# Full attention in a four-stage transformer kernel: rows of tiles taken from last to first, sums of masked values made beforehand, and masks and normalisation moved to GpSimd

## The reference

```python
def _scaled_dot_product_attention(q, k, v):
    scores = jnp.einsum('bqd,bkd->bqk', q, k) / jnp.sqrt(jnp.float32(d_k))
    scores = jnp.triu(scores, k=0)
    scores = jnp.where(scores == 0, MASK_NEG, scores)      # -9e15
    attn = jax.nn.softmax(scores, axis=-1)
    return jnp.einsum('bqk,bkd->bqd', attn, v)
x = x + _L0_attn_b_ref(_layernorm(x, axis=-1), L0_attn_b_W)      # one head of 128
# _L0_ffn_ref, routing part
probs = jax.nn.softmax(xf @ w_router, axis=-1)
topk_w, topk_idx = jax.lax.top_k(probs, TOP_K)
```

## Time and profile before

| what | us |
|---|---|
| median of three runs | 1597.03 |
| profiled execution | 1602.1 |
| its span, first to last instruction | 1600.3 |
| TensorE busy, 9684 matmuls | 1295.0 (81%) |
| VectorE busy | 1071.1 (67%) |
| ScalarE busy | 909.5 (57%) |
| GpSimd busy | 789.2 (49%) |
| norm 2: first transfer to the first projection of the attention | 1055.14 to 1097.13 |
| full attention, first projection to first load of the experts | 1097.13 to 1396.68 |

### The profile page before, as it was taken

One profiled execution on the slowest core, in us unless ns is written; L12 is line 12 of the kernel. 1 busy time (PEld: TensorE's weight loads), 2 busy tenths in 40 slices (PEclk: granted clock), 3 DMA queues, 4 the chain that ended last, 5 costly groups with the idle time before them and its releaser, 6 DMA issues. The chain is left out here.

```text
span 1600.3 us, 34684 instructions
## 1 busy us (share of the span) xinstructions
PE 1295.0 (81%) x9684; PEld 1015.8 (63%) x9684; DVE 1071.1 (67%) x3751; ACT 909.5 (57%) x2312; POOL 789.2 (49%) x814
## 2 busy tenths in 40 slices
PE   0699999999999999999982888916977886188891
PEld 0467666766766776676661888903765666188890
DVE  5666776877877788776864455556886878445563
ACT  1277777768777686767752544513764666044450
POOL 4357667676676857757672354510022223434451
PEclk9899999999999999999995989957999899598996
DMA  5699995000000000000004112130000000121215
GB/s 191 117 206 198 204 203 107 1 7 7 4 11 0 15 1 7 8 2 13 1 14 135 56 57 59 55 105 0 1 14 14 14 18 25 35 65 52 62 55 158
DMA packets 129390, 91.84 MB, mean 57 GB/s; under 512 B 9115, under 2 KB 122030, under 8 KB 128992
## 3 DMA queue, kind: packets, MB, share of 16 engines
q1 hardware_dynamic: 118848, 71.32, 20.3%
q0 software_dynamic: 9248, 16.94, 3.2%
q10 hardware_dynamic: 1152, 2.13, 0.4%
HBM read 30.86 MB, written 61.64 MB: 58 GB/s over the span
## 5 line engine op out<-in xcount | busy, mean ns | idle before, releaser
L812 DVE CUSTOM_DVE_ANT_0 sc<-ps,mask 128x256 f32<-128x256 f32 x518 | 198.6, 420 | 161.4 <-PE ps L627 137.8
L734 ACT ACTIVATE sc<-sc,mx 128x256 f32<-128x256 f32 x516 | 256.9, 501 | 40.0 <-DVE mx L812 39.4
L962 POOL TENSOR_TENSOR rot<-rot,sin 128x512 f32<-128x512 f32 x132 | 183.6, 1391 | 191.0 <-DVE rot L821 191.0
L1109 POOL DMA_INDIRECT yt<-yo,xt x160 | 160.3, 1002 | 197.5 <-DVE yo L1209 167.4
L441 POOL DMA_INDIRECT xg<-r_xw,r_slot x128 | 127.2, 994 | 170.7 <-DVE r_slot L418 136.1
L742 ACT COPY pT<-pt 128x512 f32<-128x512 f32 x257 | 150.1, 584 | 103.2 <-PE pt L637 95.2
L627 PE MATMUL ps<-K,Q 64*128 64x256 f32 x1036 | 193.1, 435 | 15.2 <-DVE mx L812 15.2
L1169 ACT ACTIVATE hT<-ph,b 128x256 f32<-128x256 f32 x320 | 125.4, 475 | 86.5 <-PE ph L1132 86.5
L637 PE MATMUL pt<-ident,sc 128*128 128x128 f32 x1028 | 171.3, 290 | 1.5 <-ACT sc L734 1.3
L650 PE MATMUL po<-pT,V 128*64 128x128 f32 x2048 | 171.5, 289 | 0.0
L637 PEld LDWEIGHTS pt<-ident,sc 128*128 128x128 f32 x1028 | 109.7, 142 | 86.2 <-issue 57.6
(11 more groups left out here) (236 smaller groups left out, 2767.9 us busy)
## 6 DMA issues: line engine op xcount, KB each, us to landing
xg<-zeros SPq DMA_DIRECT2D x76, 520.0 KB, 10.8
xt<-xg SPq DMA_DIRECT2D x80, 130.0 KB, 2.1
got<-yt SPq DMA_DIRECT2D x32, 256.0 KB, 4.5
yt<-yo,xt POOLq DMA_INDIRECT x160, 2.3
x<-in_hidden SPq DMA_DIRECT2D x8, 256.0 KB, 8.1
xg<-r_xw,r_slot POOLq DMA_INDIRECT x128, 2.3
w<-in_w SPq DMA_DIRECT2D x1, 2048.0 KB, 8.7
out_x<-x SPq DMA_DIRECT2D x8, 256.0 KB, 4.0
```

The costliest lines, as they stand in the source:

```text
L734: nc.scalar.activation(sc[:, b, h, :], sc[:, b, h, :], ACT.Exp, scale=-1.0, bias=mx[:, b, h:h + 1], accum_out=ls[:, c % 2, b, h:h + 1]).th ...
L812: nc.vector.tensor_tensor_reduce(sc[:, b, h, :], ps[:, h, 0:2 * P], (mask0 if b == 0 else mask)[:, :], -float(HD) ** -0.5, 3e38, ALU.add, ...
L962: nc.gpsimd.tensor_tensor(rot[:, which, :], rot[:, which, :], s.sin[:, pos(sb)], ALU.mult).then_inc(S["pool"], 1)
L1109: nc.gpsimd.indirect_dma_start(out=s.yt, out_offset=bass.IndirectOffsetOnAxis(ap=xt[:, k, r, HID:HID + 1].bitcast(U32), axis=0), in_=yo[:, ...
```

## The change

Five things change, nearly all in the full attention.

- Rows run from the last to the first: r = 0 is row i = 15, with one tile. The groups of 512 tokens are finished and routed from the last to the first of each sequence (`where`). ROUTE_AT is set anew.
- The sums of masked values are made once per batch, before the rows. TensorE makes four products of ones with all the values (projections 12 to 15), VectorE adds them up to the sums `pre` of all 16 rows (`sums`). TensorE adds a row's part to `bpo` by one product of `diag`, the identity times the weights `w0`, with `pre`. VectorE's `finish` is a reciprocal and an update straight from PSUM.
- GpSimd masks the first tile of a row (`mask`) and makes `diag` (`weigh`), with waits on ScalarE's copy and weights; VectorE's take then waits for the mask. With one chunk in a row the second reduction is left out.
- GpSimd normalises a group for the routing (`normalise_on_pool`); VectorE only sends the reciprocal (`invert`). Its scatters are spread over four chunks, two at a time.
- Two groups share a semaphore for fetched outputs, so `combine` waits for the transfers of both.

```diff
-            sp.dma_start(got[:, k, r, :], parts[k][:, r, :]).then_inc(s.fetched[i], 16)
+            sp.dma_start(got[:, k, r, :], parts[k][:, r, :]).then_inc(s.fetched[i // 2], 16)
...
-    ch.eng.wait_ge(s.fetched[i], 16 * TOPK * nth)
+    ch.eng.wait_ge(s.fetched[i // 2], 32 * TOPK * nth)
...
-        return self.s.x[:, bass.ds(g * SB_TILES + t, 1), :].rearrange("p o d -> p (o d)")
+        return self.s.x[:, bass.ds(self.where(g) * SB_TILES + t, 1), :].rearrange("p o d -> p (o d)")
...
+    def invert(self, dve, g):
+        self.hold(dve, self.S["std"], START + g + 1)
+        self.nc.vector.reciprocal(self.rstd[:, :], self.tmp[:, 0, :]).then_inc(self.S["rs"], 1)
+
+    def normalise_on_pool(self, pool, g):
+
+        pool.wait_ge(self.S["rs"], START + g + 1)
+        if g >= self.bufs:
+            pool.wait_ge(self.put[self.buf(g)], 16 * TOPK * SB_TILES * (g // self.bufs))
+        for t in range(SB_TILES):
+            ins = self.nc.gpsimd.tensor_scalar(self.xw[:, self.buf(g), 0, t, 0:HID], self.tile(g, t),
+                                               self.mean[:, t:t + 1], self.rstd[:, t:t + 1], ALU.subtract, ALU.mult)
+        ins.then_inc(self.S["xn"], 1)
...
-        rt = Router(nc, m, s, 3, 2, 0)
+        rt = Router(nc, m, s, 3, 2, 0, lambda j: BTILES // SB_TILES * (j // 4) + 3 - j % 4)
...
-        pre = m.sb("pre", [P, HID + 1])
-        oo = m.sb("oo", [P, HID + 1])
+        pre = m.sb("pre", [P, BTILES, HID + 1])
+        diag = m.sb("diag", [P, DBUF, P])
...
-        chunks = [[(k, min(4, BTILES - k)) for k in range(i, BTILES, 4)] for i in range(BTILES)]
-        first = [sum(len(c) for c in chunks[:i]) for i in range(BTILES + 1)]
+        rows = [(BTILES - 1 - r, [(k, min(4, BTILES - k)) for k in range(BTILES - 1 - r, BTILES, 4)])
+                for r in range(BTILES)]
+        first = [sum(len(chunks) for _, chunks in rows[:r]) for r in range(BTILES + 1)]
         NCH = first[-1]
...
         ROUTE_AT = [first[4 * j % BTILES + 4] + 1 + NCH * (j // 4) for j in range(NSB)]
-        ROUTE_AT[3], ROUTE_AT[7] = NCH + 5, 2 * NCH + 2
-        END, MORE = 2 * NCH, 9
-        STATS, ROOT, NORMALISE, TURN, LOGITS, EXPS, CHOOSE, SUM, COUNT, SLOTS = 0, 0, 1, 2, 3, 3, 4, 5, 6, 6
+        ROUTE_AT[3], ROUTE_AT[4], ROUTE_AT[5], ROUTE_AT[7] = NCH + 3, NCH + 10, NCH + 17, 2 * NCH + 1
+        END, MORE = 2 * NCH, 12
...
+                for a in range(16):
                     if a >= 2:
-                        k = min(a - 1, 8)
-                        pe.wait_ge(S["qk"], START + 8 * b + k)
-                        if a - 1 > 8:
-                            pe.wait_ge(S["v"], START + 4 * b + a - 9)
+                        pe.wait_ge(S["qk"], START + 8 * b + min(a - 1, 8))
+                    if 10 <= a < 14:
+                        pe.wait_ge(S["v"], START + 4 * b + a - 9)
+                    if a >= 14:
+                        pe.wait_ge(S["pre"], START + 4 * b + a - 13)
                     if a < 2:
-                        pe.wait_ge(S["pre_sb"], START + (BTILES - 1) * b)
+                        pe.wait_ge(S["pre"], START + 4 * b)
+                    if a == 12:
+                        pe.wait_ge(S["v"], START + 4 * (b + 1))
+                        for g in range(AHEAD):
+                            scores(g)
                     sl = slice(a % 4 * SB, (a % 4 + 1) * SB)
                     if a < 8:
...
+                    elif a >= 12:
+                        g = a % 4 * SB_TILES
+                        ins = nc.tensor.matmul(pp[:, a % 2, :], s.ones[:, :], V[:, g:g + SB_TILES, 0:HID],
+                                               start=True, stop=True)
...
+                        ins = nc.tensor.matmul(po[:, r % 2, 0:HID + 1], pT[:, g % 2, t, :], V[:, k0 + t, :],
+                                               start=(c == 0 and t == 0), stop=False)
+                    if c == len(rows[r][1]) - 1:
+                        pe.wait_ge(S["pre"], START + 4 * (b + 1))
+                        pe.wait_ge(S["diag"], START + BTILES * b + r + 1)
+                        ins = nc.tensor.matmul(po[:, r % 2, 0:HID + 1], diag[:, r % DBUF, :], pre[:, i, :],
+                                               start=False, stop=True)
                     ins.then_inc(S["pv"], 1)
 
...
-                    i, c, _, _ = chunk[g]
-                    if c == 0 and i > 0:
-
-                        pe.wait_ge(S["pre_sb"], START + (BTILES - 1) * b + max(i - 2, 0))
-                        nc.tensor.matmul(pp[:, i % 2, 0:HID + 1], s.ones[:, :], V[:, i - 1, :], start=True,
-                                         stop=True).then_inc(S["pre"], 1)
...
-                    ch.wait()
+                    dve.wait_ge(S["o"], START + 4 * (j + 1))
...
-                    rt.normalise(dve, j)
+                    rt.invert(dve, j)
...
+                def sums(a):
+
+                    dve.wait_ge(S["proj"], START + 16 * b + a + 1)
+                    for t in range(SB_TILES):
+                        i = a % 4 * SB_TILES + t
+                        if i < BTILES - 1:
+                            ins = nc.vector.tensor_tensor(pre[:, i + 1, 0:HID], pre[:, i, 0:HID],
+                                                          pp[:, a % 2, t * P:(t + 1) * P], ALU.add)
+                            ch.link(ins)
+                    dve.sem_inc(S["pre"], 1)
...
+                    if c == 0:
+                        dve.wait_ge(S["tri"], START + 2 + BTILES * b + r + 1)
                     to = U[:, g % UBUF, 0:n * P]
-                    if c == 0:
-
-                        ch.link(nc.vector.tensor_tensor(to[:, 0:P], to[:, 0:P], tri[:, :], ALU.mult))
...
+                    last = c == len(rows[r][1]) - 1
+                    least = mn[:, r % UBUF, c:c + 1]
+                    ins = nc.vector.tensor_reduce(least, to, AX_X, ALU.min)
...
+                def finish(r):
+
+                    i = rows[r][0]
+                    dve.wait_ge(S["pv"], START + NCH * b + first[r + 1])
+                    ch.link(nc.vector.reciprocal(st[:, r % UBUF, 3:4], po[:, r % 2, HID:HID + 1]))
                     own = s.x[:, b * BTILES + i, :]
-                    ch.mark(nc.vector.scalar_tensor_tensor(own, oo[:, 0:HID], st[:, i % UBUF, 3:4], own,
-                                                           ALU.mult, ALU.add))
+                    nc.vector.scalar_tensor_tensor(own, po[:, r % 2, 0:HID], st[:, r % UBUF, 3:4], own,
+                                                   ALU.mult, ALU.add).then_inc(S["o"], 1)
...
                     take(g)
+                for a in range(12, 16):
+                    sums(a)
...
+                    rt.normalise_on_pool(pool, j)
+                    rt.second(pool, j)
+                for t in range(SB_TILES):
+                    for j in at(b, g, SCATTER + t):
+                        rt.scatter(pool, j, (t,))
+
+            for b in range(BATCH):
+                def mask(g):
+
+                    r, i, c, k0, n = chunk[g]
+                    if c == 0:
+                        pool.wait_ge(S["copy"], START + NCH * b + g + 1)
+                        of = U[:, g % UBUF, 0:P]
+                        nc.gpsimd.tensor_tensor(of, of, tri[:, :], ALU.mult).then_inc(S["tri"], 1)
+
+                def weigh(g):
+
+                    r, i, c, k0, n = chunk[g]
+                    if c == 0:
+                        pool.wait_ge(S["w0"], START + BTILES * b + r + 1)
+                        if BTILES * b + r >= DBUF:
+                            pool.wait_ge(S["o"], START + BTILES * b + r - DBUF + 1)
+                        nc.gpsimd.tensor_scalar(diag[:, r % DBUF, :], s.ident[:, :], st[:, r % UBUF, 2:3], None,
+                                                ALU.mult).then_inc(S["diag"], 1)
+
+                for g in range(AHEAD - 1):
+                    mask(g)
+                weigh(0)
+                for g in range(NCH):
+                    if g + AHEAD - 1 < NCH:
+                        mask(g + AHEAD - 1)
+                    if g + 1 < NCH:
+                        weigh(g + 1)
+                    route(b, g)
+            for g in range(NCH, NCH + MORE):
+                route(1, g)
             rt.scattered(pool)
 
```

115 lines of the change are left out of this document (48 added, 67 removed).

## The result

The changed kernel takes 1644.9 us by the median of four runs, against 1598.6 us before in the same session: a ratio of 1.0292, 95% interval 1.0257 to 1.0327. (One of the four was a disturbed run of 4155.4 us; the other three are 1638.2 to 1645.7, and the ratio rests on these.) The direction was forecast, +46 us instead of +16 was not, and 1645 lies outside the range that ended at 1629.

What follows compares the result with a forecast made beforehand. In full attention TensorE was taken to set the pace in undisturbed rows, time coming only from batch starts, routing stops and tail. Terms 10.8 + 4.3 + 3.6 - 0.9 - 6.0 + 4.2 = +16.0 on 1597.0 gave 1613 us, range 1588 to 1629.

Steps and rivals of the forecast that it cites:

- (a): Start of a batch: TensorE's first transpose comes 5.4 us later in each of two batches, +10.8 us.
- (c): Stops at routing: shorter root, count and slot stops against GpSimd's normalisation and new places of routings, +3.6 us in sum.
- (b): Work inside the loops: nine more tiles of scores in each loop, diagonal products replacing ones products, +4.3 us.
- The price of a routing in long rows: Full attention: root stop 3.53 us, half clock 1.6, count wait 2.1, slots about 0.8; called about 8.4 us.
- (e): Between batches: the projections no longer wait for the running sum, -0.9 us.
- (d): Masks and weights on GpSimd: masks taken at 0.5 us, weights 0.3, with slack to spare, so 0 us.
- (f): Tail behind the last value product: less row work ahead of the last group's statistics, -6.0 us.
- (g): One semaphore for two groups of fetched results: later adds in the norm stage and at the end, +4.2 us.
- The second, GpSimd as the bound: Rival: GpSimd ends each routing late, eight routings cost 2 us each, +16, 1629 us; chance 0.12.
- the two signs that I named against myself: Prediction wrong if loops take less than 101 and 109 us, or if VectorE's takes wait for masks.
- The first, VectorE as what TensorE waits for: Rival: count and slot stops go, roots shrink, less half clock, start with +2.5; 1587 us; chance 0.22.
- The third: Rival: shorter routing stops keep the clock, 1.6 us go in each of seven routings, -11, 1602 us; chance 0.18.

Runs made afterwards that it cites:

- e6: Against e3, the 15 sums of a batch's start moved between VectorE's first takes, two ones products ahead of TensorE's first scores: 1613.5 us.
- e11: e3 plus sums moved as in e6, later routing steps, and separate signals for the first and last fetched groups: 1604.6 us.
- e1: The changed kernel with the four normalisation passes of a group back on VectorE: 1623.9 us.
- e3: The changed kernel with both masks and normalisation back on VectorE; GpSimd keeps weights, second copy and spread scatters: 1614.8 us.
- e2: The changed kernel with the 32 masks back on VectorE, normalisation and weights staying on GpSimd: 1640.2 us.
- e10: e3 with rows from first to last and routings where the kernel before the change has them: 1609.6 us.
- e9: The changed kernel with routing steps further apart: root one chunk later, turning two chunks behind normalisation, count and slots three later: 1620.1 us.

## Why the prediction was wrong, step by step

**(a) start, +10.8: right** (+12.0). The first transposes came 28.7 and 25.5 us after the first projections, 27.5 and 25 forecast, behind two ones products that waited 3.7 us for VectorE at the most. Its condition also showed: the second of them runs at the lower clock (1.19 and 1.06 us for its two halves, 0.59 undisturbed), in the second batch both. What the step lacked is that in reversed rows this time is not for sale; e6 and e11 moved it into the loops.

**(c), the term "GpSimd normalises, +0.5 at each turning, +3.5": this is the step that failed.** Measured: the waits for the turning go from 2.9 to 23.9 us in the loops, and giving the normalisation back takes 16.8 us out of the loops and 2.2 out of the tail (e1). Two things were mis-sized. The pass costs 0.84 us (0.78 with nothing beside it), not 0.29 to 0.5: I took a copy and a share of a two-input product for an operation that the trace of before did not have on GpSimd, a product with two operands per partition, and called them bounds. By the nearest row I should have let the upper bound go to the whole 1.39 us of the earlier trace rows, not its share per element. And I added a difference of durations where the chain wanted the whole: TensorE asks one chunk behind the reciprocal, so all 3.4 us of the passes stand open less what the root's own stop covers. On top of the waits comes the lower clock behind each. With 3.4 instead of 1.1 us and a start 0.1 later the sum would have had +2.4 for each of seven, 16.8 in place of 3.5, and 1626 us. That this is what e1 took out of the loops to the tenth is luck.

The loops' 26 us add up by e1 and e3: normalisation 16.8 where 3.5 stood, masks 6.9 where 0 stood, and all the rest of the change 9.2 (226.9 in e3, 217.7 before) where 3.5 stood.

**(c), the rest.** Count stops were to shrink by 0.7 each and did not: in the loops 2.4 us each after, 2.1 before. Choosing the experts is untouched, and VectorE reaches it late. The roots' stops shrank nearly as forecast (18.4 us in seven before, 15.4 after, 14.6 in e10; -4.2 forecast). The new places of the routings were priced too low: with the additional scores of (b) the reversed order was to cost 13.1 us in the loops (3.9 + 9.2), and between e10 and e3 it is 23. Each of these is one trace. The price of a routing in long rows has a slip of its own: its terms (3.53, 1.6, 2.1 and 0.8) add up to 8.0 us, not 8.4, which would have made (c) +2.0; the 12 us for short rows have no row behind them.

**(b) +4.3 and (e) -0.9** can't be read off as times; the reversed loops hold the additional scores, and the projections of the second batch start without a wait.

**(d) masks and weights, 0: wrong by 6 to 9 us** (e1 to e3), and invisible while the normalisation is there (e2). The mask's own price was right. VectorE's two-input pass of 512 elements took 703 ns instead of 689 on average, so contention lengthened its 56 passes by 0.8 us in all at most. The Trainium skill (GPSIMD Engine Reference, Key points) says that GpSimd shares its SBUF interfaces with VectorE and contends with instructions that have two SBUF inputs. This trace shows it small on VectorE's side; what it shows on GpSimd's stands in the last section. By the waits the cost is the hand-over: the pass waits for a mask that waits for ScalarE's copy, with GpSimd's own queue between.

**(f) tail, -6.0: -4.4**, with 2.2 of GpSimd's normalisation in it (e1), which I had at 0.5; without it the step was right.

**(g) +4.2: +1.5.** 2.5 in the norm stage and -1.0 in the last one, where later adds run together. The first add comes 6.3 us behind the first fetch, 6.7 forecast.

**The rivals.** The second, GpSimd as the bound, at 0.12, was the nearest: VectorE's takes do wait for masks, 37.5 us in 13 places. Of the two signs that I named against myself this one came; the other, loops shorter than 101 and 109 us, did not, and I had named none for loops of 122 and 128, which is where the error was. But the rival's mechanism, masks late behind scatters, is the smaller part; the larger is GpSimd's own passes on the path. The first, VectorE as what TensorE waits for, is false for this kernel. Its forward version has shorter loops, but the stops that this rival wanted gone are still there: 12.6 us ahead of the count in e10, 12.4 before. The third fell, though three of the root's stops did shrink to 1.3 or 1.4 us: behind each of them GpSimd's passes set a second stop, of 2.7 to 3.7 us.

## What to carry over

An operation that no row of the trace has on an engine is not bounded by its cheapest relative there; when four of them stand one step ahead of the engine that sets the pace, count their whole time, and the slower clock behind the new stop. Before moving work to another engine, ask which step needs the result next, and whether a chunk more of distance costs anything (e9: 21 us of the attention back without moving an instruction to another engine). And take a bundled change apart before judging it: this one lost 46 us, while its better half in forward rows won 5, and 15 with the routing's steps further apart.
